# Waits of the exp instructions on ScalarE in an attention kernel: one pair of waits for every two steps, set one step tighter, in place of a pair for each step

## The reference, cut to what matters

```python
xn = _layernorm(x, axis=-1)
q = (xn @ Wq.T + bq)   # 16 heads of 64, and k, v likewise
scores = jnp.einsum('bhqd,bhkd->bhqk', q, k) * (1.0 / np.sqrt(64))
attn = jax.nn.softmax(scores, axis=-1)
out = jnp.einsum('bhqk,bhkd->bhqd', attn, v)
y = real(ifft(fft(xn) @ w)) + bias
x = x + out @ Wo.T + bo + y
```

## Time and profile before

| | us |
|---|---|
| time before, median of 2 runs | 4125.23 |
| lowest and highest of them | 4100.72, 4149.73 |
| the profiled execution's own time | 4103.06 |
| its span on the slowest core (core 3) | 4101.2 |
| spans of the eight cores | 4078.8 to 4101.2 |

### The profile page before, as it was taken

How to read it: one execution, slowest core, us unless ns; L and a number is a source line. 1 busy time by engine, 2 the same in 40 slices (tenths; PEclk the granted TensorE clock), 3 DMA queues, 4 the chain that set the end, 5 groups by cost and what they waited for, 6 DMA issues and landing times.

```text
span 4101.2 us, 48985 instructions; the slowest of 8 cores (4078.8 to 4101.2 us)
## 1 busy us (share of the span) xinstructions
PE 2659.0 (65%) x12224; PEld 881.7 (21%) x12224; DVE 2212.6 (54%) x3167; ACT 2163.0 (53%) x2146; POOL 234.6 (6%) x444
## 2 busy tenths in 40 slices
PE   1147797889666576646665675667476656656664
PEld 0113343334222122212211221122122112211221
DVE  5741133333477367727754773677267637744773
ACT  1210000000688288828855893788188638846882
POOL 1000112101000100000000001000100000010000
PEclk9998898999899689969976996899599859977996
DMA  3221133211300430060015003400510160025003
GB/s 99 77 48 25 41 135 93 61 21 70 126 1 1 98 98 1 13 155 28 1 33 163 1 1 71 125 1 1 135 60 1 23 173 1 1 56 145 1 1 77
DMA packets 96008, 231.88 MB, mean 57 GB/s; under 512 B 12736, under 2 KB 12752, under 8 KB 95744
## 3 DMA queue, kind: packets, MB, share of 16 engines
q0 software_dynamic: 45056, 111.29, 11.8%
q1 hardware_dynamic: 50688, 117.46, 9.0%
HBM read 220.32 MB, written 52.43 MB: 67 GB/s over the span
## 4 chain that ended last, share of the span: by engine, by line
ACT 25%; DVE 16%; PE 14%; DMA 10%; issue 8%; ACTq 1%; DVEq 1%; SPq 0%; POOLq 0%; POOL 0%
ACT a L904 12%; ACT pt2t L904 7%; DMA wo_sbt<-woT 6%; ACT xstaget L904 6%; DVE rcptt L942 5%; DVE a L927 5%; PE pOu L811 4%; DMA bigA<-v_scr 4%; PE pSA L780 2%; PE pSB L780 2%; DVE a L925 1%; DVE zf32t L940 1%; PE pSA L881 1%; DVE a L964 1%; DVE a L961 1%
## 5 line engine op out<-in xcount | busy, mean ns | idle before, releaser
L904 ACT ACTIVATE a<-pSA,lnbiast 128x1024 f16<-128x1024 f32 x512 | 584.0, 1141 | 733.4 <-PE pSA L785 573.6
L927 DVE TENSOR_TENSOR a<-a 128x1024 f16<-128x1024 f16 x896 | 620.2, 692 | 296.3 <-ACT a L904 280.6
L780 PE MATMUL pSA<-a,bigB 64*128 64x512 f16 x1024 | 426.6, 417 | 463.0 <-ACT a L904 275.5
L904 ACT ACTIVATE pt2t<-pSA,lnbiast 128x1024 f16<-128x1024 f32 x512 | 580.5, 1134 | 99.5 <-PE pSA L785 97.5
L904 ACT ACTIVATE xstaget<-pSB,lnbiast 128x1024 f16<-128x1024 f32 x512 | 581.4, 1136 | 14.8 <-PE pSB L785 14.5
L904 ACT ACTIVATE a<-pSB,lnbiast 128x1024 f16<-128x1024 f32 x512 | 586.3, 1145 | 4.1 <-PE pSB L785 2.3
L780 PE MATMUL pSB<-a,bigB 64*128 64x512 f16 x1024 | 422.7, 413 | 205.7 <-ACT xstaget L904 113.1
L811 PE MATMUL pOu<-a,bigA 128*64 128x512 f16 x1024 | 452.8, 442 | 47.3 <-DMA bigA<-v_scr 43.1
L816 PE MATMUL pOu<-a,bigA 128*64 128x512 f16 x1024 | 454.4, 444 | 0.0
L927 DVE TENSOR_TENSOR a<-a,xstaget 128x1024 f16<-128x1024 f16 x512 | 354.4, 692 | 158.6 <-ACT xstaget L904 146.3
L927 DVE TENSOR_TENSOR a<-a,pt2t 128x1024 f16<-128x1024 f16 x512 | 354.3, 692 | 156.4 <-ACT pt2t L904 143.2
(11 more groups left out here) (141 smaller groups left out, 3493.8 us busy)
## 6 DMA issues: line engine op xcount, KB each, us to landing
bigA<-v_scr SPq DMA_DIRECT2D x256, 256.0 KB, 3.5
a<-x SPq DMA_DIRECT2D x64, 512.0 KB, 4.3
wo_sbt<-woT POOLq DMA_DIRECT2D x128, 256.0 KB, 4.8
part_scr<-a POOLq DMA_DIRECT2D x32, 512.0 KB, 2.9
a<-part_scr POOLq DMA_DIRECT2D x32, 512.0 KB, 6.9
out<-a SPq DMA_DIRECT2D x32, 512.0 KB, 4.5
q_scr<-qstaget POOLq DMA_DIRECT2D x64, 128.0 KB, 2.1
v_scr<-vstaget POOLq DMA_DIRECT2D x32, 256.0 KB, 2.3
```

The lines of the kernel that those rows point to most:

```text
L780: te.matmul(sset[:, 0:512], KT[0:64, pr * T + kc * 128:pr * T + (kc + 1) * 128], QTs[0:64, pr * 512:(pr + 1) * 512], start=True, stop=True)
L904: AC.inc(sc.activation(PT[u % 4], SA[u % 2][:], AF.Exp, bias=lnbias, scale=0.125))
L927: DV.inc(v.tensor_add(PS[kc % 2], PS[kc % 2], PT[u % 4]))
```

## The change

Only ScalarE's waits in the attention block are edited. The first four steps of a slice (u = 0 to 3) keep theirs. From u = 4 on, an even step waits for `pv(u-3)` and the sum of step u-3 in place of `pv(u-4)` and the sum of step u-4. An odd step waits for its scores alone. The counts still protect the buffers: the even step ahead of an odd step u waits for step (u-1)-3 = u-4, which is what the odd step needs.

```diff
                     for u in range(NP * NKC):
                         sc.wait_ge(semTE, teM[(q, "sc", u)])
                         if u >= 4:
-                            sc.wait_ge(semTE, teM[(q, "pv", u - 4)])
-                            sc.wait_ge(semDV,
-                                       dvM[("ps", (u - 4) // NKC,
-                                            (u - 4) % NKC)])
+                            if u % 2 == 0:
+                                sc.wait_ge(semTE, teM[(q, "pv", u - 3)])
+                                sc.wait_ge(semDV,
+                                           dvM[("ps", (u - 3) // NKC,
+                                                (u - 3) % NKC)])
                         elif q > 0:
                             sc.wait_ge(semTE, teM[(q - 1, "pv", 252 + u)])
                             sc.wait_ge(semDV, dvM_prev[("ps", 7, 28 + u)])
```

## The result

| | before | after |
|---|---|---|
| median of all runs, us | 4117.39 (42 runs) | 4125.6 (43 runs) |
| lowest, highest | 4099.42, 4220.27 | 4114.31, 4230.57 |
| ratio to before | | 1.0036, interval 1.0021 to 1.0052 |
| span of the profiled execution | 4101.2 | 4121.4 |

The change makes the kernel 0.36% slower, which is 15 us of some 4110 (8.6 to 21.4), against a forecast of 28 us on the profiled time. The predicted 4131 lies 5 us above the median of the changed kernel. Measured again beside the experiments, the ratio is 1.0056 (1.0032 to 1.008).

A forecast was written before the change was run, and what follows sets the result against it. The prediction took a chain of ScalarE exp steps to bound the attention block, with stalls at 56 pair boundaries where ScalarE waits for VectorE's copy. 4103.1 + 29.7 - 1.9 gave 4131 us, range 4108 to 4178.

The forecast's parts named there:

- The tighter wait at kc 4: At 56 pair boundaries, the exp of kc 4 waits for VectorE's second copy, 0.53 us later each, 29.7 us in all.
- rival D: Behind a boundary, something other than the exp chain holds the stretch and absorbs the shift; time stays 4103; chance 0.05.
- The tighter waits elsewhere: At other even steps and on `pv`, the tighter waits cost nothing; slack in the steady stretch is 1.0 us.
- The removed waits: On odd steps, 2016 of 4032 waits go; gain 1.9 us from fewer gaps that look like instruction refills.
- a quarter of the entries goes away, so 16 of 64 such gaps would: One 0.12 us exp gap per pair, read as an instruction refill; 16 of 64 vanish, 1.9 us gained.
- Rival C: Removed waits gain only where exps start right behind them, in the low-clock stretch; 12 us less, 4119; chance 0.08.
- Rival A: Behind boundaries, longer idle time stretches TensorE's low-clock stretch to twice as long; 23 us more, 4154; chance 0.12.
- Rival B: On all 1008 odd steps the removed waits are worth 0.11 us each; 111 us off, 4022; chance 0.03.
- The sign and the class: Whole kernel: slower, +0.7%; chance 0.96 for within 2%, 0.02 for over 2% slower, 0.02 for over 2% faster.

The follow-up runs named there:

- e1: Against before: the change's tighter waits on even steps, all three waits kept on odd steps; ratio 1.0102, die span +31 us.
- e2: Against before: only the exp of kc 4 in pairs 1 to 7 waits one step tighter (56 steps); ratio 1.0098, die span +31 us.
- e9: The change's waits put on e8, the kernel with VectorE's boundary work thinned; ratio 0.966, 40 us slower than e8.
- e3: The change, except that kc 4 and kc 5 of pairs 1 to 7 wait for u-4 as before; ratio 0.9978, die span 12 us less than before.
- e5: Against before: only the wait for pv(u-4) left out in every step, 2016 waits fewer, nothing tightened; ratio 0.9989, die span 9 us less.
- e4: The changed kernel itself, measured again on the chip of e1 to e3; ratio 1.0056 to before, die span +18 us.
- e6: Against before: ScalarE's two protecting waits written twice, 4032 entries more, nothing tighter; a single run at 4132.84 us, 28 us over before's median, no ratio.
- e8: Against before: waits unchanged, a pair's reciprocal (in two halves) and cast on VectorE moved into the next pair; ratio 0.9563, profiled span 3928.0.
- e7: Against before: the change on the other parity, odd steps wait for u-3 and even steps for their scores alone; ratio 1.0108, die span +44 us.

## Why the prediction was right or wrong

**The tighter wait at kc 4, +29.7 us: right in place, mechanism and size.** The idle time grew by 28.0 us in 56 places, the median of a pair's kc 0 to 4 grew by 0.53 us (9.85 to 10.39), and the runs that carry this edit and nothing else read +31. The second copy is the releaser, 0.53 us later, and nothing behind it absorbed the shift (rival D fell).

**The tighter waits elsewhere, nothing: right.** e1 and e2 read the same. e9 shows the condition: the slack of about 1 us in the steady stretch holds only as long as no other VectorE work of 1.73 us stands in it.

**The removed waits, -1.9 us: right in sign and far too small.** They give 12 us (e3) or 9 us (e5), and e1 against e4 gives 13. That is the term that makes the forecast of +28 too high: 31 - 12 is 19, and the two ratios say 15 and 23. What failed is the step "a quarter of the entries goes away, so 16 of 64 such gaps would". The loss did not go down with the number of entries; at full clock it nearly vanished, from 7.0 to 1.6 us. With fewer waits in a step ScalarE's instructions stand ready earlier (the recorded duration of an exp grows to 1.27 us, where it stopped at 1.22 in before), and most gaps no longer reach the engine. This reading fits e3, e5 and e6 and was not tested by itself. The remaining 3 to 7 us stay open: e4 against e1 has them spread over all other places.

That the 4131 lies 5 us from the median of the changed kernel is in part luck. The forecast of the difference was 13 us too high (28 for 15), and it was added to an execution of 4103 us, 14 us under the median of before.

**Rival C, exps that start right behind their waits, 12 us: right in size, not in place.** Its place was the low-clock stretch. By number it was the nearest, 4119 for 4103.1 x 1.0036 = 4118, but for another reason. In its stretch the change gained 1 to 2 us (474 to 473) and TensorE kept the pace, as I had argued. But e6 shows that the margin is thin. With 0.11 us more in a step, the same stretch loses 13 us.

**Rival A, the clock: fell at its place, and open at another.** The stretch behind the boundary did not grow. But behind the end of a pair more exps came late. In before, 18 of 448 exps of kc 2 (all cores) ended more than 3.7 us after the one ahead. In the change it was 58 of 448. One of them (core 3):

```profile
2291.10 0.59 PE L830 MATMUL pzb<-a,zselt 128*2 128x512 f16 x1 [1.01 <-DVE scltt L933]
2291.48 0.63 PE L832 MATMUL pzb<-a,zselt 128*2 128x512 f16 x1
...
2293.72 1.11 ACT L905 ACTIVATE pt2t<-pSA,lnbiast 128x1024 f16<-128x1024 f32 x1 [2.82 <-PE pSA L785]
```

Here the sums over partitions take 0.6 us a matmul, the granted clock of 2289.5 to 2293.5 is 0.70, and ScalarE idles 2.82 us where 1.75 is usual. 40 more of these in eight cores at 1.07 us are 5 us per core. That is most of what kc 0 to 4 grew by in the table beyond the 30 of kc 4 (36 in all). All of the traces with the tight step at kc 4 show it (56 to 85 of 448), e3 and e5 do not (19 and 26). But e6 and e8, where nothing is tighter, have 50 and 44, and the +31 of e1 and e2 leaves about 1 us for it beside the 29.7. So it is not shown to be a cost of the change.

**Rival B, every wait worth its time: fell.** e3 and e5 give a tenth of its 111 us, and e6 adds 4032 waits for 28 us, 7 ns each. Where ScalarE stands waiting a wait has its price: the step of kc 2 is 2.87 us in before, 2.98 with two waits more (e6) and 2.81 with one fewer (e5). The 50 to 100 ns that the Trainium skill gives for reading a semaphore ("Advanced Engine Details and Errata", Network/Comms) agree with these 0.05 to 0.06 us for one. At full clock the waits lie behind the exp ahead.

**The sign and the class.** "Slower by less than 2%" held. My 0.96 for within 2% was well placed.

## What to carry to other kernels

A rule such as "wait for two steps at once, every other step" costs one instruction of the waited-for engine wherever that engine is behind (0.53 us here), or a whole step of the waiting engine if it holds a step that had not been held (1.01 us in e7), and nothing elsewhere. So look for the places where the releaser is late and count them, before looking at the steady stretch. Wait instructions on an engine that runs back to back are nearly free, 7 ns each in e6. When a wait is long, the cure is the work that makes the releaser late, here a reciprocal that nobody needed for another 30 us.

## What the runs showed of the hardware

- A wait instruction costs 0.05 to 0.06 us where the engine starts directly behind it (kc 2 in e5 and e6). At full clock, five in a step of 1.005 us cost nothing visible except in 1 step of 19 or so, which takes 1.23 us. They only shorten the lead of the exps: the duration grows to 1.15 us with five waits, to 1.22 with three and to 1.27 in the change.
- The instruction queue brings one packet for about 126 entries (147 against 131 for 2016 fewer, 178 for 4032 more). A step of ScalarE that takes 1.13 us in place of 1.005 came once per 128 entries in before, always at the same kc.
- A reciprocal over 2 partitions takes 3.34 us for 512 elements and 1.73 us for 256 (e8).
